# Criss-cross attention on one core: the residual added by accumulating transfers, column groups that overwrite the accumulators, smaller packets for queries and keys

## The reference: what is computed

```python
q = einsum('bchw,oc->bohw', x, Wq) + bq      # x: [8, 512, 96, 96]; 64 rows of q and k, 512 of v
k = einsum('bchw,oc->bohw', x, Wk) + bk
v = einsum('bchw,oc->bohw', x, Wv) + bv
eH = einsum('bchw,bcpw->bhwp', q, k)         # along the column; the diagonal is masked
eW = einsum('bchw,bchp->bhwp', q, k)         # along the row
att = softmax(concatenate([eH, eW], axis=3), axis=3)
outH = einsum('bcpw,bhwp->bchw', v, attH)
outW = einsum('bchp,bhwp->bchw', v, attW)
return gamma * (outH + outW) + x
```

## Time and profile before

| | |
|---|---|
| Runs | 4565.44, 4566.75, 4570.79 us; median 4566.75 |
| The profiled execution | 4574.0 us, its span 4572.2 us |
| One image in steady state | start to start 555.7 us ((4211.2 - 321.1) / 7, from the copy of line 888 that opens each) |
| PE busy | 3525.7 us (77%) |
| DVE busy | 2972.1 us (65%) |
| Moved by the transfers | 1179.38 MB, mean 258 GB/s |

### The profile page before, as it was taken

One profiled execution on the slowest core, in us unless ns is written; L12 is line 12 of the kernel. 1 busy time (PEld: TensorE's weight loads), 2 busy tenths in 40 slices (PEclk: granted clock), 3 DMA queues, 4 the chain that ended last, 5 costly groups with the idle time before them and its releaser, 6 DMA issues.

```text
span 4572.2 us, 96032 instructions
## 1 busy us (share of the span) xinstructions
PE 3525.7 (77%) x33624; PEld 2418.0 (53%) x33624; DVE 2972.1 (65%) x4282; ACT 1716.7 (38%) x3660; POOL 506.9 (11%) x691
## 2 busy tenths in 40 slices
PE   3986888678876778767788678886787868877676
PEld 2543565445654556545565355563565635655565
DVE  6746775476764866639666386574775747856576
ACT  2434442353423534235242352433433334333431
POOL 0000120001200022000210002100031000300210
PEclk9997798887998789887899878997698986989577
DMA  7967779976889669896698876988769987799489
GB/s 283 299 184 237 245 239 296 290 232 231 271 274 309 211 232 281 264 299 219 217 311 268 272 250 192 338 267 250 261 186 318 292 235 252 204 317 290 148 256 298
DMA packets 753781, 1179.38 MB, mean 258 GB/s; under 512 B 50800, under 2 KB 568432, under 8 KB 744048
## 3 DMA queue, kind: packets, MB, share of 16 engines
q1 hardware_dynamic: 434256, 831.89, 57.7%
q10 hardware_dynamic: 319008, 340.88, 23.1%
HBM read 832.83 MB, written 339.74 MB: 256 GB/s over the span
## 4 chain that ended last, share of the span: by engine, by line
issue 72%; PE 9%; POOL 9%; DVE 4%; DMA 4%; ACT 1%; SPq 1%; POOLq 0%; ACTq 0%; DVEq 0%
POOL qk_lo L455 3%; POOL prob_col L473 3%; POOL prob_row L473 2%; DVE acc L835 2%; PE banks L967 2%; PE banks L969 2%; PE banks L968 2%; DMA v_in<-v_pixel_major 1%; DMA acc<-x 1%; PE banks L1035 1%; DMA out<-acc 1%; PE banks L1037 1%; PE banks L1036 1%; DMA x_first<-x 1%; SPq L361 1%
## 5 line engine op out<-in xcount | busy, mean ns | idle before, releaser
L835 DVE SCALAR_TENSOR_TENSOR acc<-banks,att,acc 128x384 f32<-128x384 f32 x1536 | 1130.0, 797 | 198.9 <-DMA acc<-x 127.2
L967 PE MATMUL banks<-wv_hi,x_hi 128*128 128x512 f16 x2304 | 929.1, 403 | 395.6 <-DVE x_lo L757 394.9
L765 DVE SCALAR_TENSOR_TENSOR v_out<-banks,proj,v_out 128x512 f16<-128x512 f32 x576 | 431.5, 749 | 1134.1 <-ACT v_out L559 1133.5
L968 PE MATMUL banks<-wv_lo,x_hi 128*128 128x512 f16 x2304 | 923.7, 401 | 0.0
L969 PE MATMUL banks<-wv_hi,x_lo 128*128 128x512 f16 x2304 | 919.3, 399 | 0.0
L559 ACT ACTIVATE v_out<-banks,proj 128x512 f16<-128x512 f32 x576 | 390.3, 682 | 859.6 <-PE banks L969 829.2
L1035 PE MATMUL banks<-prob_col,v_in 96*128 96x96 f16 x3072 | 465.5, 214 | 242.1 <-DVE acc L835 236.1
L455 POOL TENSOR_TENSOR qk_lo<-qk_f,qk_hi 128x256 f16<-128x256 f32 x288 | 193.3, 671 | 3567.0 <-ACT qk_hi L567 3559.4
L967 PEld LDWEIGHTS banks<-wv_hi,x_hi 128*128 128x128 f16 x2304 | 235.5, 102 | 663.5 <-issue 456.3
L1035 PE MATMUL banks<-prob_row,v_in 96*128 96x96 f16 x3072 | 456.3, 213 | 101.9 <-DMA v_in<-v_pixel_major 49.8
L1007 PE MATMUL banks<-k_hi,q_both 128*96 128x96 f16 x1536 | 365.1, 295 | 212.4 <-ACT prob_row L606 164.8
(11 more groups left out here) (100 smaller groups left out, 6374.2 us busy)
## 6 DMA issues: line engine op xcount, KB each, us to landing
v_in<-v_pixel_major SPq DMA_DIRECT2D x768, 384.0 KB, 6.0
x_raw<-x ACTq DMA_DIRECT2D x290, 512.0 KB, 7.2
x_next<-x SPq DMA_DIRECT2D x192, 768.0 KB, 4.3
v_pixel_major<-v_out ACTq DMA_DIRECT2D x576, 256.0 KB, 4.0
out<-acc SPq DMA_DIRECT2D x384, 384.0 KB, 10.6
acc<-x SPq DMA_DIRECT2D x192, 384.0 KB, 12.6
acc<-x SPq DMA_DIRECT2D x8, 4608.0 KB, 13.7
acc<-x SPq DMA_DIRECT2D x16, 2304.0 KB, 18.9
```

Of the source, the lines that this page charges most:

```text
L765: nc.vector.scalar_tensor_tensor(out=v_out[tile % V_OUT][:, :, 1, :], in0=bank[tile % 2][:, :].rearrange("p (t c) -> p t c", t=CT), scalar ...
L835: nc.vector.scalar_tensor_tensor(out=a, in0=out_bank[g % OUTS], scalar=att[:, O_FACTOR:O_FACTOR + 1], in1=a, op0=ALU.mult, op1=ALU.add,).t ...
L967: nc.tensor.matmul(dst, s_hi, m_hi, start=(t == 0), stop=False)
L968: nc.tensor.matmul(dst, s_hi, m_lo, start=False, stop=False)
```

## The change

- **Residual.** The loads of the residual before and within the T stage are gone, as are ACT's bias instructions. After the row groups of a chunk, POOL issues a transfer that reads the chunk of x and adds it to the accumulator (`accum_op=ALU.add`), 48 per image; SP's store waits for it. POOL issues it two groups behind (RES_LAG), SP stores 14 groups behind instead of 6 (STORE_LAG).
- **Columns.** The column groups write acc = bank * factor + bias and don't read the accumulator. ACT does those of tt = 0, DVE those of tt = 1. Row groups stay as they were, on DVE. The first column groups wait for the scores (the accumulators hold queries and keys) or, in the second half, for all stores of the first.
- **Queries and keys.** 48 loads of 1152 pixels (2304 bytes in a partition) instead of 12 of 4608 (9216 bytes). The two halves are stored with one transfer instead of two. Chunks of the scan are loaded as two transfers of 768 columns.
- **Order.** HEAD 18 to 20 items, STATS 14 to 6, and 70 items instead of 64 in the T stage: 30 beside each half instead of 27, TURN still ten.

```diff
-    HEAD = 18
-    STATS = 14
+    QK_PIECES = 8
+    HEAD = 20
+    STATS = 6
-    STORE_LAG = 6
+    RES_LAG = 2
+    STORE_LAG = 14
...
+                for w in range(0, SCW, SCW // 2):
+                    sp.dma_start(
+                        x_next[c % NXT][:, w:w + SCW // 2], x_scan[batch, :, c * SCW + w:c * SCW + w + SCW // 2]
+                    ).then_inc(x_next_loaded[c % NXT], 16)
...
-                for c in range(2):
-                    px = slice(c * HW // 2, (c + 1) * HW // 2)
+                for piece in range(QK_PIECES):
+                    c = piece * 2 // QK_PIECES
+                    px = slice(piece * HW // QK_PIECES, (piece + 1) * HW // QK_PIECES)
                     sp.dma_start(q_both[0:CQ, px], qk[b, 0, 0:CQ, px]).then_inc(qk_loaded[c], 16)
...
-                sp.wait_ge(bias_added, b * (CT * NCH) + tp * (TT * NCH) + (h // 2) * TT + tt + 1)
+                sp.wait_ge(res_added[tt][h // 2], b * (TP * 16) + tp * 16 + 16)
...
-                sp.dma_start(acc[0][:, :], x_acc[b, 0, :, :]).then_inc(acc_loaded[0], 16)
-                sp.dma_start(acc[1][:, 0:HW // 2], x_acc[b, 1, :, 0:HW // 2]).then_inc(acc_loaded[1], 16)
...
+            def add_residual(b, g):
+                tp, o, h, tt = group_at(g)
+                px = slice(h // 2 * CH, (h // 2 + 1) * CH)
+                pool.wait_ge(row_added, b * (GROUPS // 2) + row_number(g) + 1 + ONE0)
+                pool.dma_start(
+                    acc[tt][:, px], x_acc[b, tp * TT + tt, :, px], accum_op=ALU.add
+                ).then_inc(res_added[tt][h // 2], 16)
...
-                act.dma_start(qk[m, 0, :, px], qk_hi[n % 2][:, :]).then_inc(qk_stored[n % 2], 16)
-                act.dma_start(qk[m, 1, :, px], qk_lo[n % 2][:, :]).then_inc(qk_stored[n % 2], 16)
+                act.dma_start(qk_store[m, :, :, px], qk_pair[n % 2][:, :, :]).then_inc(qk_stored[n % 2], 16)
...
-            def add_bias(b, g):
+            def evacuate_column(b, g):
                 tp, o, h, tt = group_at(g)
...
+                if h == 0 and tp > 0:
+                    for c in range(NCH):
+                        wait_alone(act, out_stored[tt][c], b * (TP * 16) + tp * 16 + 16)
+                act.wait_ge(o_mm, b * GROUPS + g + 1 + ONE0)
                 nc.scalar.activation(
-                    acc[tt][:, px], acc[tt][:, px], ACT.Identity, bias=gbv_col[:, tp * TT + tt:tp * TT + tt + 1]
-                ).then_inc(bias_added, 1)
+                    acc_strips[tt][COL][:, h * G:(h + 1) * G, :], out_bank[g % OUTS], ACT.Identity,
+                    scale=att[:, O_FACTOR:O_FACTOR + 1], bias=gbv_col[:, tp * TT + tt:tp * TT + tt + 1],
+                ).then_inc(col_act, 1)
...
+                nc.vector.tensor_scalar(
+                    acc_strips[tt][COL][:, h * G:(h + 1) * G, :], out_bank[g % OUTS], att[:, O_FACTOR:O_FACTOR + 1],
+                    gbv_col[:, tp * TT + tt:tp * TT + tt + 1], ALU.mult, ALU.add,
+                ).then_inc(col_dve, 1)
```

More of the change, by code:

```diff
@@ L146, in criss_cross_attention @@
     qk_f32, _ = place("qk_f32", [P, BLK], F32)
-    qk_hi = [place(f"qk_hi{s}", [P, BLK], F16)[0] for s in range(2)]
-    qk_lo = [place(f"qk_lo{s}", [P, BLK], F16)[0] for s in range(2)]
+    qk_pair = [place(f"qk_pair{s}", [P, 2, BLK], F16)[0] for s in range(2)]
     v_in = [place(f"v_in{u}", [L, G, TT, 2, P], F16)[0] for u in range(VU)]
@@ L248, in criss_cross_attention @@
         o_mm = sem("o_mm")
-        acc_loaded = [sem(f"acc_loaded{tt}") for tt in range(TT)]
-        acc_added = sem("acc_added")
-        bias_added = sem("bias_added")
+        col_act = sem("col_act")
+        col_dve = sem("col_dve")
+        row_added = sem("row_added")
+        res_added = [[sem(f"res_added{tt}_{c}") for c in range(NCH)] for tt in range(TT)]
         out_stored = [[sem(f"out_stored{tt}_{c}") for c in range(NCH)] for tt in range(TT)]
-        QK_MM0, V_READY0, QK_READY0, SPLIT0, E0, P0, ADDED0, ONE0 = 2, 2, 2, 2, 2, 2, OUTS, 1
+        QK_MM0, V_READY0, QK_READY0, SPLIT0, E0, P0, ONE0 = 2, 2, 2, 2, 2, 2, 1
         CHAIN = 7
@@ L286, in group_at, with row_number, col_number @@
             return i // HALF, (COL, ROW)[i // (NG * TT) % 2], i // TT % NG, i % TT
+        def row_number(g):
+            return g // HALF * (HALF // 2) + g % HALF - HALF // 2
+        def col_number(g):
+            return g // HALF * NG + g % HALF // TT
         def strips_at(j):
@@ L401, in batch @@
                                 store_chunk(b, last)
[L402 to L409, removed]
             with sp.Fori(0, SCAN // FIRST) as i:
@@ L501, in batch @@
                             normalise(b, g // TT + LA)
+                        if g % HALF >= RES_LAG:
+                            tp, o, h, tt = group_at(g - RES_LAG)
+                            if o == ROW and h % 2:
+                                add_residual(b, g - RES_LAG)
+                        if g % HALF == HALF - 1:
+                            for last in range(g - RES_LAG + 1, g + 1):
+                                add_residual(b, last)
             reduce_xmax(0)
@@ L514, in _ @@
             act.sem_inc(e_ready, E0)
+            act.sem_inc(col_act, ONE0)
             act.wait_ge(w_scale_chain, 4)
@@ L646, in batch @@
                             high_parts(b, g // TT + AHEAD)
[L647 to L651, removed]
-                            for last in range(g - SETTLE + 1, g + 1):
-                                if group_at(last)[2] % 2:
-                                    add_bias(b, last)
+                        if o == COL and tt == 0:
+                            evacuate_column(b, g)
                 if items:
@@ L923, in batch @@
                             low_parts(b, g // TT + AHEAD)
-                        add_group(b, g)
+                        if o == ROW:
+                            add_row(b, g)
+                        elif tt == 1:
+                            evacuate_column(b, g)
                 if items:
@@ L1029, in attend @@
                     pe.wait_ge(v_loaded[u], b * (ROUNDS["load"] * 16) + (load // VU + 1) * 16)
-                pe.wait_ge(acc_added, b * GROUPS + i - OUTS + 1 + ADDED0)
+                if i >= OUTS:
+                    before = i - OUTS
+                    if group_at(before)[1] == ROW:
+                        pe.wait_ge(row_added, b * (GROUPS // 2) + row_number(before) + 1 + ONE0)
+                    else:
+                        emptied = col_dve if group_at(before)[3] else col_act
+                        pe.wait_ge(emptied, b * (TP * NG) + col_number(before) + 1 + ONE0)
                 dst = out_bank[i % OUTS]
```

69 lines of the change are left out of this document (32 added, 37 removed).

## The result

The changed kernel takes 4591.46 us (median of five runs, 4583.45 to 4596.20) against 4568.74 for the kernel before (five runs). The ratio is 1.0048, 95% interval 1.0033 to 1.0063: half a per cent slower, where I had forecast 2.4% faster. The time lies in the stated range, on the other side of no change.

What follows compares the result with a forecast made beforehand. Transfer engines were taken to fill both row phases, while HEAD, STATS and the column phases had room. Terms of -18 us per image, -126 for seven, and +20 for the last gave 4461 us; stated range 4360 to 4740.

Steps and rivals of the forecast that it cites:

- the price of an accumulate beyond a plain load: Transfer engines: adding to the accumulator costs 8 us per image more than a load that overwrites; bounds 0 and 53.
- The first rival: Both row phases: an accumulate costs about twice a load; 4613 us at half price to 4821 at full; chance 0.27.
- my signs of being wrong: Row phases growing over 45 us together, or PE waiting at the first score pair for queries and keys.
- HEAD: Start of an image: shorter query and key packets shrink the stall of x; 70 us for 76, -6.
- The rival that HEAD gains nothing: HEAD: the stall of x is spread out, not removed; HEAD stays at 80 us, total 4531; chance 0.13.
- STATS: Between scores and column groups: eight items and the residual's loads leave; 18 us for 52, -34.
- First column phase: First half's column groups: ACT relieves DVE, PE alone in front with 1.5 more items; stays at 75 us, 0.
- Second column phase: Second half's column groups: waits for the reload and for DVE end; 62 us for 73, -11.
- Second row phase: Second half's row groups: 24 accumulates, 9.4 MB, join the transfers; 85 us for 63, +22.
- POOL's queue: Rival: accumulates in POOL's in-order queue hold up queries and keys, 48 us per image, about 4800 us; chance 0.05.
- The last image: Final image, without items: first column phase -18, second half +20, last add +10, accumulate price +8; together +20.
- The row phases not bound by transfers: Second row phase: accumulates fit in at 5 us rather than 22; 4286 us, or 4370 at half; chance 0.11.

## Why the prediction was wrong, point by point

**The step that failed is the price of an accumulate beyond a plain load.** I bounded it by 0 and 53 us per image and took 8, "since that row is the same transfer but for the second read". The changed kernel against the one with plain loads gives 553.7 - 514.6 = 39 us per image and 39 in the last. Put into the sum in place of 8, this alone gives 4461 + 7 x 31 + 31 = 4709. That is too slow, because the other terms came out better, by 15 us per image and 16 in the last: 4709 - 7 x 15 - 16 = 4588, against 4591 measured. So the time lies inside the stated range only because two errors of opposite sign nearly cancel. The row I leaned on couldn't answer: here a landing time says little about the engine time that a transfer takes. The accumulates land sooner (10.0 us) than the reloads did (12.6), and yet each takes 1.91 times the engine time of a plain load. These are the transfers of the changed kernel and then of the one with plain loads, and PE's wait in the latter:

```profile
v_in<-v_pixel_major SPq DMA_DIRECT2D x768, 384.0 KB, 7.2
...
acc<-x POOLq DMA_DIRECT2D x384, 384.0 KB, 10.0
out<-acc SPq DMA_DIRECT2D x384, 384.0 KB, 15.2
```
```profile
v_in<-v_pixel_major SPq DMA_DIRECT2D x768, 384.0 KB, 7.3
...
acc<-x POOLq DMA_DIRECT2D x384, 384.0 KB, 7.4
out<-acc SPq DMA_DIRECT2D x384, 384.0 KB, 14.1
...
PE banks L1061 <- DMA v_in<-v_pixel_major: 167.3, 97, 5.5
```

Even the median landing of v's tiles is the same in both; only PE's wait for them (394 and 167 us) and the queue's share show the price.

With the row phases at a share of 1.00 to 1.06, added engine time had to be priced as time: it came through as 20 us in the first row phase and 17 in the second. The first rival said this and was given 0.27. It was right in the doubled price and in its place. Its half price (27 us extra) gave 4613, 22 us above the result, but that nearness is partly luck: the real extra is nearer to 40, and the other terms made up for it.

Of my signs of being wrong, one came: the two row phases grew by 21 + 34 = 55 us together, more than the 45 that I had set. The landing misled as a sign. I had written 13 us for plain accumulates and over 20 for doubled ones, and they landed in 10.0 although their price was doubled. So did the length of the second row phase, about 85 or over 105 us: it is 90, and 74 with plain loads.

**The other terms**, per image, plain loads against before (first table):

- HEAD: forecast -6, measured -14.5 (-12 with accumulates). The longest wait for x fell to 6.2 us in the fourth image, as said. I held that the bytes would set the length, and the share is 1.01 to 1.04; but a full share now carries 316 to 327 GB/s where 0.89 carried 244, and the engine time of the queries' and keys' own packets fell by a fifth. The rival that HEAD gains nothing falls.
- Scores: forecast 0, measured +4 to +5. The cause is open. In the table the two versions of the changed kernel with long packets or without the residual are at 105.5 and 105.9, near the 104.4 of before.
- STATS: forecast -34, measured -29. The chain up to the factor is 15 us instead of 13, the rest 8 instead of 5.
- First column phase: 0, measured -3. The column instructions were mis-sized (650 ns for 945 and 1022), but DVE and ACT had room.
- First row phase and TURN: +3, measured +0.7 (+20.6 with accumulates).
- Second column phase: -11, measured -13 (-17 with accumulates).
- Second row phase: +22, measured +17 (+34 with accumulates).

Sum for plain loads: forecast -26, measured -41. So without the add the arithmetic from bytes, rates and PE's steps held within 5 us for every stage but HEAD. For STATS the number held, but the run with the old order shows that the items make only 18.5 us of it.

**POOL's queue.** An accumulate holds POOL 0.99 us each, but DVE waited 5 us in all for the low half of the keys, and PE's wait for POOL's scaling is 59 us, with plain loads 60. It costs nothing, as forecast; that rival falls.

**The last image**: forecast +20, of which 8 for accumulates; measured +35, and -4 with plain loads. Its first column phase gave 26 us rather than 18.

**The row phases not bound by transfers**: the rival falls. With plain loads the second is 17 us longer for its 9.4 MB, with accumulates 34.

**Where the gain went** (us, from the runs): short packets 113 and order of items 110, each undone by itself in the changed kernel. The version with plain loads, which has all of the change but the add, gains 4569 - 4268 = 301 in all, and the adding takes 323 back.

## What to carry to other kernels

Before work is moved from a compute engine to the transfer engines, look at their share in the very stage where it would run. In these row phases, at a share of 1.0 or more, 375 us of added time per engine made the kernel 323 us longer, and an accumulating transfer took as much of it as two plain ones (1.91). Judge such a price by the queue's share, not by the landing. Where two queues meet, try shorter packets on the one that isn't urgent. When a bundle of edits ends near zero, run its parts one by one: here parts worth 2% each were hidden by one that took them back.

## What the runs showed of the hardware that I had not expected

- An accumulating load of 128 x 768 fp32 took 32.7 us of engine time summed over the 16 engines, a plain one on the same queue 17.1, while its landing is only 10.0 us against 7.4. Its packets carried 3072 bytes and took 255 ns on average; SP's packets of 3072 bytes in the same kernel took 137.
- The issue of an accumulate takes POOL 0.99 us on average, of a plain load 0.55.
- Loads of 64 partitions with rows of 2304 bytes took less engine time than with rows of 9216: 124 ns a packet against 623, so 54 ns for each 1000 bytes against 68. HEAD of the kernel before ran at 298 instead of 244 GB/s.
- An evacuation from PSUM to an accumulator with a step of 96 elements takes DVE 945 ns and ACT 1022 ns for 384 columns. DVE's takes 953 when it reads the accumulator too, and 609 if it reads it and there is no step.
